# A transformer block on one core: the prologue in another order, with two pairs of PSUM banks for head 0's maxima

## The reference, cut to what matters

```python
x = x + attn_a(layernorm(x))   # 16 heads of 64, causal, x is (2, 1024, 128), with biases bq, bk, bv, bo
x = x + ffn(layernorm(x))      # 128 -> 512 -> 128, relu
x = x + attn_b(layernorm(x))   # one head of 128, causal, with an ALiBi bias
x = x + ffn(layernorm(x))

# attn_a, for each of the 2 x 16 heads:
q = x @ Wq[h] + bq[h];  k = x @ Wk[h] + bk[h];  v = x @ Wv[h] + bv[h]
scores = q @ k.T / 8, masked above the diagonal
out_h = softmax(scores) @ v;   result = concat(out_h) @ Wo + bo
```

## Time and profile before

| | us |
|---|---|
| median of 3 runs | 609.73 (609.67 to 610.58) |
| the profiled execution's own time | 613.79 |
| its span in the profile | 612.0 |
| TensorE busy in the span | 563.1 (92%) |
| GpSimd busy | 398.8 (65%) |

### The profile page before, as it was taken

The page is one execution under the profiler, slowest core; times in us unless marked ns, Lnnn a source line. Parts: engine busy times, 40 slices in busy tenths (PEclk is TensorE's granted clock), DMA queues, the critical chain, the costliest instruction groups (busy, mean ns, idle before and its releaser), DMA issues.

```text
span 612.0 us, 16889 instructions
## 1 busy us (share of the span) xinstructions
PE 563.1 (92%) x6384; PEld 418.9 (68%) x6384; DVE 470.7 (77%) x1442; ACT 462.0 (75%) x877; POOL 398.8 (65%) x380
## 2 busy tenths in 40 slices
PE   2778999899999999999999999989899998889797
PEld 2755677667777677777777776766788776667575
DVE  5556888788888888888888888874378798588774
ACT  3637889989998998999899889988455883165375
POOL 3449898878888888888888888889510231066310
PEclk9988999999999999999999999999899997599799
DMA  9432234233343333324424333313661000000001
GB/s 215 98 85 53 54 95 97 62 81 87 98 95 88 87 85 92 106 58 109 107 61 111 82 89 87 82 60 112 244 206 70 2 0 1 0 2 1 2 18 52
DMA packets 35329, 47.90 MB, mean 78 GB/s; under 512 B 10776, under 2 KB 16688, under 8 KB 35248
## 3 DMA queue, kind: packets, MB, share of 16 engines
q1 hardware_dynamic: 33136, 46.29, 28.3%
q10 hardware_dynamic: 2112, 0.54, 0.5%
HBM read 12.21 MB, written 9.44 MB: 35 GB/s over the span
## 4 chain that ended last, share of the span: by engine, by line
PE 67%; DVE 9%; issue 8%; ACT 7%; POOL 1%; DVEq 0%; ACTq 0%; POOLq 0%
PE psum L525 8%; PE psum L581 8%; PE psum L582 8%; PE psum L481 7%; PE psum L483 6%; PE psum L482 6%; PE psum L563 5%; PE psum L561 5%; PE psum L562 5%; PE psum L733 2%; PE psum L584 2%; ACT p L996 2%; PE psum L795 1%; DVE xn L1117 1%; ACT p_hl L997 1%
## 5 line engine op out<-in xcount | busy, mean ns | idle before, releaser
L1563 POOL TENSOR_TENSOR p_hl<-p,p_hl 128x512 f16<-128x512 f32 x288 | 327.1, 1160 | 52.3 <-ACT p_hl L997 51.3
L1149 DVE CUSTOM_DVE_ANT_0 max_junk<-psum,mask_s 128x1024 bf16<-128x1024 f32 (+7 forms) x256 | 190.5, 753 | 39.7 <-issue 39.4
L996 ACT ACTIVATE p<-psum 128x512 f32<-128x512 f32 x288 | 176.9, 614 | 18.6 <-PE psum L584 14.7
L997 ACT ACTIVATE p_hl<-psum 128x512 f16<-128x512 f32 x288 | 177.9, 618 | 0.0
L561 PE MATMUL psum<-v_all,p_hl 128*128 128x65 f16 x1152 | 125.7, 194 | 2.5 <-POOL p_hl L1563 2.5
L581 PE MATMUL psum<-q_hl,k_hh 128*128 128x512 f16 (+3 forms) x384 | 125.9, 328 | 0.5 <-ACT p_hl L997 0.4
L562 PE MATMUL psum<-v_all,p_hl 128*128 128x64 f16 x1152 | 125.8, 193 | 0.0
L563 PE MATMUL psum<-v_all,p_hl 128*128 128x65 f16 x1152 | 125.4, 195 | 0.0
L582 PE MATMUL psum<-q_hm,k_l 128*128 128x512 f16 (+3 forms) x384 | 122.3, 327 | 0.0
L561 PEld LDWEIGHTS psum<-v_all,p_hl 128*128 128x128 f16 x1152 | 107.8, 98 | 17.3 <-POOL p_hl L1563 2.8
L562 PEld LDWEIGHTS psum<-v_all,p_hl 128*128 128x128 f16 x1152 | 107.0, 98 | 4.8
(11 more groups left out here) (189 smaller groups left out, 1143.7 us busy)
## 6 DMA issues: line engine op xcount, KB each, us to landing
k_hh<-st_hi SPq DMA_DIRECT2D x64, 128.0 KB, 2.3
o_scratch<-o_sb SPq DMA_DIRECT2D x16, 512.0 KB, 2.6
o_in<-o_scratch SPq DMA_DIRECT2D x4, 2048.0 KB, 8.4
k_l<-st_lo SPq DMA_DIRECT2D x32, 128.0 KB, 2.4
q_hl<-st_hi SPq DMA_DIRECT2D x32, 128.0 KB, 2.3
q_hl<-st_lo SPq DMA_DIRECT2D x32, 128.0 KB, 2.4
q_hm<-st_hi SPq DMA_DIRECT2D x32, 128.0 KB, 2.4
x_sb<-in_L_attn_a_x SPq DMA_DIRECT2D x4, 256.0 KB, 4.4
```

Of the source, the lines that this page charges most:

```text
L996: nc.scalar.activation(p32[:, ring_at(u, r), :], src, ACT.Exp, scale=SCALE_A).then_inc(exp_done, 1)
L997: nc.scalar.activation(p_hl[:, u % 2, 0, BANK * r:BANK * (r + 1)], src, ACT.Exp, scale=SCALE_A).then_inc(phi_done, 1)
L1149: nc.vector.tensor_tensor_reduce(out=max_junk[:, n % 2, 0:cols], in0=max_banks(j, 0, cols), in1=mask_s[:, S - cols:S], scale=1.0, scalar=- ...
L1563: nc.gpsimd.tensor_tensor(p_hl[:, u % 2, 1, cols], p32[:, ring_at(u, r), :], p_hl[:, u % 2, 0, cols], ALU.subtract)\
```

## The change

Loads: both first chunks of x go ahead of Wk on SP's queue, and the biases ahead of Wq on ScalarE's. The zeroing of the lower halves of `k_l1` and `q_hm` goes from VectorE's start to GpSimd, after `chunk_rstd(1)` and after the masks. On VectorE `norm_kq` stands ahead of `chunk_low(0)` and `gain_kq` ahead of `chunk_low(1)`. Head 0's maxima use two pairs of banks (3-4 and 5-6), so tile n waits only for the reduction of tile n-2. V unit 3 goes to bank 7, pieces 4 and 5 to banks 0 and 1. The 24 `idle_products` ahead of the maxima and the 10 ahead of each tile are replaced by 6 after tiles 1 to 4; the 8 products for the output bias (L686, 16 passes) go from ahead of the maxima to behind tiles 5, 6 and 7. TensorE's wait for `rest_lo` 3 goes to slot 1.

```diff
     V_BANKS = (0, 1, 2, 7)
+    FIRST_MAX = (3, 5)
...
-        def max_banks(j, c0, c1):
-            first = (MAXB + (CT - 1 - j) % 2 if j < CT else MAXB) * BANK
+        def max_banks(v, j, c0, c1):
+            if v == 0:
+                first = FIRST_MAX[(QT - 1 - j) % 2] * BANK
+            else:
+                first = (MAXB + (CT - 1 - j) % 2 if j < CT else MAXB) * BANK
...
             load_x(0)
+            load_x(1)
             sp.dma_start(w_raw[:, 0, :]..., Wk...)
-            load_x(1)
...
-                if v or n:
+                if v:
                     pe.wait_ge(max_done, QT * v + (n - max_alone(j)))
+                elif n >= 2:
+                    pe.wait_ge(max_done, n - 1)
...
+                if u == 1:
+                    pe.wait_ge(rest_lo, 3)
                 products(0)
...
             for m in range(FIRST_UNITS):
-                if m < 3:
-                    pe.wait_ge(piece_lo, m + 2)
+                pe.wait_ge(piece_lo, (2, 3, 4, 4)[m])
                 values(m, V_BANKS[m])
-            pe.wait_ge(wo_in, 16)
-            for k in range(OB):
-                last = nc.tensor.matmul(bank(6)[:, 0:1], wo_raw[:, k, :], b_cols[:, 2, k:k + 1], ...)
-            last.then_inc(bo_full, 1)
-            pe.wait_ge(v_hi_done, FIRST_UNITS)
-            idle_products(24)
             pe.wait_ge(k_moved[0], 48)
             pe.wait_ge(q_moved[0], 48)
+            pe.wait_ge(inv_done, 2)
             for n in range(QT):
-                if n:
-                    idle_products(10)
                 max_tile(0, n)
                 if n in (1, 2):
-                    pe.wait_ge(piece_lo, n + 3)
-                    piece(n + 3, MISC)
+                    pe.wait_ge(v_hi_done, n)
+                    pe.wait_ge(v32_done, n)
+                    piece(n + 3, n - 1)
...
+                if 1 <= n <= 4:
+                    idle_products(6, 2)
+                if n == 5:
+                    pe.wait_ge(wo_in, 16)
+                for k in range(3 * (n - 5), min(3 * (n - 4), OB)) if n >= 5 else ():
+                    last = nc.tensor.matmul(bank(6)[:, 0:1], wo_raw[:, k, :], b_cols[:, 2, k:k + 1], ...)
+            last.then_inc(bo_full, 1)
             turn_maxima(0)
...
-            pe.wait_ge(rest_lo, 3)
...
-            act.dma_start(w_raw[:, 1, :]..., Wq...)
             for n, b in enumerate((bk, bq, bv)):
                 act.dma_start(b_rows[...], b...)
+            act.dma_start(w_raw[:, 1, :]..., Wq...)
...
-            nc.vector.memset(k_l1[DH:P, :, :].bitcast(F32), 0.0).then_inc(kl_zeroed, 1)
-            nc.vector.memset(q_hm[DH:P, :, :].bitcast(F32), 0.0).then_inc(qm_zeroed, 1)
...
             chunk_norm(1)
+            norm_kq()
             chunk_low(0)
-            norm_kq()
+            gain_kq()
             chunk_low(1)
-            gain_kq()
...
                 take_max(0, n)
-                if n in (1, 2):
-                    piece_low(n + 3)
+                if n in (2, 3):
+                    piece_low(n + 2, n - 2)
...
             chunk_rstd(1)
+            pool.wait_ge(rstd_done, 2)
+            nc.gpsimd.memset(k_l1[DH:P, :, :].bitcast(F32), 0.0).then_inc(kl_zeroed, 1)
...
+            pool.wait_ge(diag_ready, 1)
+            nc.gpsimd.memset(q_hm[DH:P, :, :].bitcast(F32), 0.0).then_inc(qm_zeroed, 1)
```

More of the change, by code:

```diff
@@ L101, in hybrid_block @@
     FIRST_BANKS = (7, 0, 1, 2)
-    V_BANKS = (0, 1, 2, 5)
+    V_BANKS = (0, 1, 2, 7)
+    FIRST_MAX = (3, 5)
     XT_BANKS = (6, 7, 7, 7)
@@ L524, in max_tile @@
                     c1 = min(c0 + BANK, cols)
-                    last = nc.tensor.matmul(max_banks(j, c0, c1), q_hl[:, s, P * j:P * (j + 1)], k_hh[:, s, c0:c1],
+                    last = nc.tensor.matmul(max_banks(v, j, c0, c1), q_hl[:, s, P * j:P * (j + 1)], k_hh[:, s, c0:c1],
                                             start=True, stop=True)
@@ L574, in scores @@
                     pe.wait_ge(mrow_done, u + 1)
-                if u == 0 and r < ST_RING:
-                    pe.wait_ge(v_hi_done, r + 1)
+                if u == 0 and r == 0:
+                    pe.wait_ge(piece_lo, 6)
                 for i, q0, n, col in units[r]:
@@ L651, in pe_slot, with idle_products @@
                 scores(u, 8)
-            def idle_products(n):
+            def idle_products(n, dst):
                 for _ in range(n):
-                    nc.tensor.matmul(bank(5)[:, 0:P], ident_b[:, :], ident_b[:, :], start=True, stop=True)
+                    nc.tensor.matmul(bank(dst)[:, 0:P], ident_b[:, :], ident_b[:, :], start=True, stop=True)
             pe.wait_ge(bias_in, 48)
@@ L661, in _ @@
             turn_chunk(0)
-            idle_products(8)
+            idle_products(8, 5)
             turn_chunk(1)
-            idle_products(8)
+            idle_products(8, 5)
             pe.wait_ge(sq_done, 4)
@@ L668, in _ @@
             nc.tensor.matmul(bank(MAXB + 1)[:, 0:4], ones[:, :], sums[:, 0:4], start=True, stop=True).then_inc(fro_full, 1)
-            idle_products(32)
+            idle_products(32, 5)
             pe.wait_ge(first_lo, 2)
@@ L677, in _ @@
                 piece(n, FIRST_BANKS[n])
-            idle_products(12)
+            idle_products(12, 5)
             pe.wait_ge(first_lo, 3)
             for m in range(FIRST_UNITS):
-                if m < 3:
-                    pe.wait_ge(piece_lo, m + 2)
+                pe.wait_ge(piece_lo, (2, 3, 4, 4)[m])
                 values(m, V_BANKS[m])
-            pe.wait_ge(wo_in, 16)
-            for k in range(OB):
-                last = nc.tensor.matmul(bank(6)[:, 0:1], wo_raw[:, k, :], b_cols[:, 2, k:k + 1], start=(k == 0), stop=(k == OB - 1))
-            last.then_inc(bo_full, 1)
-            pe.wait_ge(v_hi_done, FIRST_UNITS)
-            idle_products(24)
             pe.wait_ge(k_moved[0], 48)
             pe.wait_ge(q_moved[0], 48)
+            pe.wait_ge(inv_done, 2)
             for n in range(QT):
-                if n:
-                    idle_products(10)
                 max_tile(0, n)
                 if n in (1, 2):
-                    pe.wait_ge(piece_lo, n + 3)
-                    piece(n + 3, MISC)
+                    pe.wait_ge(v_hi_done, n)
+                    pe.wait_ge(v32_done, n)
+                    piece(n + 3, n - 1)
+                if n == 1:
+                    pe.wait_ge(v_hi_done, 3)
+                    pe.wait_ge(v32_done, 3)
+                if 1 <= n <= 4:
[3 more added lines that the diff above has]
+                for k in range(3 * (n - 5), min(3 * (n - 4), OB)) if n >= 5 else ():
+                    last = nc.tensor.matmul(bank(6)[:, 0:1], wo_raw[:, k, :], b_cols[:, 2, k:k + 1], start=(k == 0), stop=(k == OB - 1))
+            last.then_inc(bo_full, 1)
             turn_maxima(0)
@@ L904, in _ @@
         def _(act):
-            act.dma_start(w_raw[:, 1, :].rearrange("p (h d) -> p h d", h=H), Wq.rearrange("h e d -> e h d")).then_inc(wq_in, 16)
             for n, b in enumerate((bk, bq, bv)):
                 act.dma_start(b_rows[OB * n:OB * (n + 1), :], b.rearrange("(q a) d -> q (a d)", a=2)).then_inc(bias_in, 16)
+            act.dma_start(w_raw[:, 1, :].rearrange("p (h d) -> p h d", h=H), Wq.rearrange("h e d -> e h d")).then_inc(wq_in, 16)
             def chunk_high(n):
@@ L975, in _ @@
             for n in range(4, 6):
-                piece_high(n)
+                piece_high(n, n - 4)
             for which, dst in enumerate((w_hi[:, 0, :], w_hi[:, 1, :], wv_hi[:, :])):
@@ L1148, in take_max @@
                 nc.vector.memset(gate[:, n % 2:n % 2 + 1], 0.0)
-                nc.vector.tensor_tensor_reduce(out=max_junk[:, n % 2, 0:cols], in0=max_banks(j, 0, cols),
+                nc.vector.tensor_tensor_reduce(out=max_junk[:, n % 2, 0:cols], in0=max_banks(v, j, 0, cols),
                                                in1=mask_s[:, S - cols:S], scale=1.0, scalar=-3.0e38, op0=ALU.add, op1=ALU.max,
@@ L1308, in _ @@
             max_rows(0)
+            dve.wait_ge(bo_in, 16)
+            dve.wait_ge(bo_full, 1)
+            nc.vector.tensor_tensor(bo_all[:, :], bank(6)[:, 0:1], bo_sb[:, :], ALU.add).then_inc(bo_done, 1)
             for u in range(HEADS):
@@ L1524, in _ @@
             chunk_rstd(1)
+            pool.wait_ge(rstd_done, 2)
+            nc.gpsimd.memset(k_l1[DH:P, :, :].bitcast(F32), 0.0).then_inc(kl_zeroed, 1)
             pool.wait_ge(fourths_ready, 2)
+            pool.wait_ge(kl_zeroed, 1)
             pool.wait_ge(norm_done, 2)
@@ L1534, in _ @@
                                     pattern=[[-1, QT]], channel_multiplier=1).then_inc(diag_ready, 1)
+            pool.wait_ge(diag_ready, 1)
+            nc.gpsimd.memset(q_hm[DH:P, :, :].bitcast(F32), 0.0).then_inc(qm_zeroed, 1)
             pool.wait_ge(norm_done, 3)
+            pool.wait_ge(qm_zeroed, 1)
             nc.gpsimd.tensor_tensor(gains[:, 2:3], norms[:, 2:3], minus_half[:, 0:1], ALU.pow).then_inc(pow_done, 1)
```

4 lines of the change are left out of this document (removed).

## The result

| | median us | runs | ratio to before (95%) |
|---|---|---|---|
| before | 610.15 (609.67 to 610.74) | 4 | |
| changed | 603.49 (601.13 to 605.40) | 4 | 0.9889 (0.985 to 0.9927) |

Forecast were 605.2 and a range of 602.0 to 607.8. The profiled execution of the changed kernel took 605.4, that of the kernel before 613.79: 8.4 us between two single executions, 6.7 between the medians. Both are more than the forecast 4.5. The two profiled executions have the same mean granted clock, 0.965, so the clock does not explain their 8.4; the part on the prediction takes it apart.

A forecast was written before the change was run, and what follows sets the result against it. TensorE's head slots bound the kernel, so an earlier head 0 shortens it equally: 1.7 (loads less memset) + 1.0 (copies) + 1.3 (banks) + 0.5 (tie) = 4.5 us, giving 605.2 from 609.73; range 602.0 to 607.8.

The forecast's parts named there:

- Loads to L668: From x's loads to the norms' sum over partitions: 15.69 to 12.4 by loads alone, 14.0 with the memset, gaining 1.7 us.
- I take 6.4: Assumed landing time of x's chunk 1 with both chunks ahead of Wk, chosen between 5.6 and 7.3; it was 9.88.
- no blocking: Rival: VectorE and GpSimd share without loss, so L668 comes at 12.4, 1.6 us more gained, 603.6; chance 0.23 with other cheap-end costs.
- The memset on GpSimd: Zeroing `k_l1` on GpSimd holds up three of chunk 1's four L1117 on VectorE: 1.8 us added.
- Copies to the first tile: Between q/k copies and head 0's first tile of maxima: only the transfer remains, 1.0 us gained besides the loads' 1.7.
- The maxima: VectorE's eight reductions of head 0: two pairs of banks gain 1.3 us, between ends 0 and 2.5.
- the ping-pong between the banks: VectorE's 2.5 us without work in the 10.1 us of head 0's reductions, which two pairs of banks remove.
- the give-back: In head 0's maxima: 1.2 of the 2.5 us lost again, about 0.6 to low clock and 0.6 to bias products.
- The tie at 46.03: Ahead of slot 0: TensorE's wait for GpSimd's last weight split, ending beside the maxima's rows at 45.89; moving it gains 0.5 us.
- Who lags: GpSimd's first low part comes 5.2 us behind slot 0's piece, 0.9 more than before, within 1.4 of room.

The follow-up runs named there:

- Experiment 2: Kernel before with only the new order of loads (both x chunks ahead of Wk, biases first on ScalarE): median 606.78 us, ratio 0.9964.
- experiment 1: Kernel before with only the two zeroing memsets moved from VectorE to GpSimd: ratio 1.0008; 612.0 for 610.6 us at the same clock.
- experiment 8: Changed kernel with the bias products and 24 idle products put back between V units and maxima: median 603.76 us, 603.4 at the same clock.
- experiment 7: Changed kernel with 18 more idle products, after tiles 5 and 6 and ahead of slot 0's first piece: median 602.19 us, ratio to before 0.9893.
- Experiment 3: Changed kernel with tile n of head 0's maxima waiting again for the reduction of tile n-1: median 606.92 us, 2.3 us slower at the same clock.
- experiment 4: Changed kernel with TensorE's wait for `rest_lo` 3 back ahead of slot 0: median 604.72 us, 1.3 us slower at the same clock.

## Why the prediction was right, and where its sizes were off

**Loads to L668: the step that failed is "I take 6.4".** The landing of chunk 1 was taken as 6.4 and had happened by 5.03. With it the chain through chunk 1 plus blocking was put at 14.0; it was done at 12.25, 0.2 ahead of the squares. The squares' own term was right: Wk at 9.9 forecast, 10.03 measured, L668 at 12.4 forecast, 12.47 measured. So this part gave 3.2 us, not 1.7, in this profile; in the second one Wk's squares begin at 10.58 and L676 comes at 13.02, which makes it 2.7. Experiment 2 puts it at 2.8 at the same clock. For the time this is the rival "no blocking" by its number, though not by its reason.

**The memset on GpSimd** was mis-sized (1.8 against 1.36 in the four operations), and the first of the four did not run ahead as forecast, but the blocking is real, and it came out as the forecast has it where chunk 1's way is the bound (experiment 1: 1.4 us slower). In the full change it lies under the wait for Wk, with 0.2 us to spare. The Trainium skill, SBUF — State Buffer, section "Who interferes with whom", says that whoever issues first holds the shared ports for the whole instruction and the other blocks. On the blocking the trace agrees: 2.48 us beside a memset of 1.80, 1.12 without. On who goes first it does not bear the rule out as far as the rows' starts can tell: VectorE's row starts 0.02 to 0.03 us ahead of the memset's, and VectorE is the one that waits.

**Copies to the first tile.** Forecast 1.0 besides the loads' shift; measured 27.39 - 16.57 = 10.8 against 13.1, that is 2.3. Of the 2.3, 1.1 is one q copy whose issue took 1.74 in the profile before and 0.59 here, and 1.2 is the fill, which ran at half clock there. The forecast had the fill and not the stall. At full clock the fill ended level with the copies (experiment 2), and putting it back cost 0.2 with a standard error of 0.3 (experiment 8): in the mean of many executions the forecast's 1.0 for it is not shown. The stall may itself hang on the order: an issue of 1.4 to 1.8 us stands in all four profiles with the fill ahead of the maxima, and in neither of the changed kernel's two.

**The maxima.** Forecast 1.3, measured 3.0 (10.12 to 7.16), more than the forecast's upper end of 2.5. I had given 1.2 back to a low clock and to the bias products; the clock stayed up in this execution, and of all the waits 0.2 us was left, ahead of the last reduction. The 2.5 itself was too small: it took VectorE's work as 6.09 + 1.50 = 7.6, but these busy times overlap, and the whole stretch with the same ten operations took 7.16. Nor was all of the idle time the ping-pong between the banks. In the profile before, VectorE waited 1.2 us for ScalarE's high parts:

```profile
37.38 0.75 DVE L1132 SCALAR_TENSOR_TENSOR st_lo<-psum,b_kq,st_hi 128x512 f16<-128x512 f32 x1 [0.31 <-ACT st_hi L933]
...
39.92 0.75 DVE L1132 SCALAR_TENSOR_TENSOR st_lo<-psum,b_kq,st_hi 128x512 f16<-128x512 f32 x1 [0.90 <-ACT st_hi L933]
```

The change also puts both low parts one reduction later, and there they wait for nothing; no run has this part alone. The first tile, at full clock, also gave VectorE work 0.8 behind its start instead of 1.2. Where the clock was low in the maxima (experiment 7) tile 0 to the turning took 9.0 instead of 8.0: the give-back is real, but not in every execution. Experiment 3 puts the second pair of banks at 2.3 at the same clock.

**The tie at 46.03.** As forecast: without the moved wait slot 0 hangs on GpSimd's splits (experiment 4, 1.3 us).

**Who lags.** GpSimd's first low part came 5.2 behind slot 0's piece, as forecast, and delayed nobody: TensorE's idle time in slot 0 is 1.34 us in both profiles.

**What the forecast had not:** slot 0 at half clock for longer in this execution. Its piece was 9.4 us earlier, slot 1 8.5. The 9.4 is the forecast's 4.5, and 1.5 more for the loads, 1.3 for the copies, 1.7 for the reductions and 0.4 for the first tile. Over many executions it is less: 7.4 us at the same clock, 5.6 in the means of all runs, 6.7 in the first medians. The parts measured alone come near the 7.4: 2.8 (loads), 2.3 (second pair), 1.3 (moved wait) and 0.2 (fill) make 6.6, with a standard error of 0.6. So the way was right, and in the profile its three larger terms (loads, copies, maxima) were each too small. That 4.5 lies near the 5.6 of the means is partly luck: the mean clocks of the two kernels, and with them 1.8 us, were no part of the forecast.

## What to carry to other kernels

Moving work off an engine that waits is not free if the new engine shares ports with it at the wrong moment; look at what the other one runs in the same microsecond, and then whether that way is the bound at all. When a chain is shortened from the front, read which of its two inputs lands last after the edit, not before: here the landing of Wk took over from the landing of x. And where executions scatter by more than the effect, put each time beside its mean granted clock before trusting a difference of medians; then look in the trace where the low clock lies before blaming the part that was changed.

## What was not expected of the hardware

The time of one and the same kernel goes with the mean granted clock at a correlation of -0.93 (54 executions of the kernel before, 605.7 to 612.3 us). In the profiles up to 10 us of the low clock lie in the first 60 us, and 19 to 36 behind the last head's maxima, in code that is the same in all of them. In the first part TensorE was at 1.2 GHz ahead of the maxima, in them, in slot 0, in several of these or in none, for some 3 to 7 us at a time, and slot 0, from its first piece to slot 1, lasted from 10.6 to 13.1 us. In the changed kernel the clock fell at 35.8, after TensorE had waited for the narrow tiles' reductions (PE busy 0.38 of the us from 32.0 and 0.68 of the next). And the issue of one 128 KB copy on SP's queue takes 0.6 us, or, once among the first twelve of a run, 0.8 to 2.1: in all four profiles of kernels with the bias products and the fill ahead of the maxima (1.4 to 1.8), and in three of the other ten. No run shows why.
